# A segment-memory attention kernel: the memory update's products join the read-outs' transactions, the pair loop is written out, and Q and K are stored in runs of 8

## The chip, the core and the metric

The kernel runs on one core of a Trainium2 chip. Its engines are TensorE (PE, which multiplies and transposes), VectorE (DVE), ScalarE (ACT), GpSimd (POOL) and SyncE (SP, which issues DMAs). They run side by side and wait for each other through semaphores. The metric is the device time of one execution in microseconds, less is better.

## What is computed

A transformer block: attention with a memory carried over segments, then a coupled feed-forward net. The work around the change is the attention (input (8, 512, 256), 16 heads of 64, segments of 128 rows):

```python
def step(carry, seg):
    M, Z = carry
    scores = jnp.einsum('bhid,bhjd->bhij', q, k) * scale
    scores = jnp.where(mask, -jnp.inf, scores)
    att_dot = jnp.einsum('bhij,bhjv->bhiv', jax.nn.softmax(scores, axis=-1), v)
    sq = jax.nn.elu(q) + 1.0
    att_mem = sq @ M / (sq @ jnp.swapaxes(Z, -2, -1))
    sk = jax.nn.elu(k) + 1.0
    M_new = M + jnp.einsum('bhld,bhlv->bhdv', sk, v)
    Z_new = Z + sk.sum(axis=-2, keepdims=True)
    att = gate * att_mem + (1.0 - gate) * att_dot
    out = att.reshape(B, LSEG, H * DV) @ Wo
    return ((M_new, Z_new), out)
```

Before it stand a layer norm and the projections of x by Wq, Wk and Wv; behind it a layer norm and the residual sum. Then comes a feed-forward net over three cycles, again with norm and residual.

## The kernel before

The eight sequences are worked in four pairs, each over four segments: 16 steps (bp, s). One step handles 32 units (2 sequences x 16 heads) in 4 groups of 8. For pairs 0 to 2 each engine runs a loop (`Fori`) whose body holds the four steps of a pair; the last pair is written out behind it, without the parts that prepare further segments.

The order of the work is written by hand, as a function `step` for each engine, and each engine executes its own list in order. For each group g a step has `turn` (PE transposes the pairs of heads of Q and K), ACT's `take_q` and DVE's `take_q` (split into two f16 parts, and elu of Q), `scores` (PE, L1140 and L1145), `maxima` (DVE, L837), `probs` (ACT, eight exps, L576), `turn_probs` (PE, L1156), `take_p` (ACT, L582), two `read_out` halves (PE, L1169 for probabilities times V, L1174 for elu(Q) times memory), `divide` (DVE, L844 and L847) and `gated` (POOL, L420 to L424). Beside them the six projections of the next segment run (`project`, PE, L1111, 12 matmuls each). DVE turns each result in blocks from PSUM into Q, K or V (`take_x`, L816). The attention of the previous step is turned (`to_rows`, DVE, L913; `turn_att`, PE, L1201) and multiplied by Wo (`project_out`, PE, L1216, 32 matmuls); its norms are `y_norm` and `x2_norm` (DVE, L760), with POOL's `deviation` (L390, L392). N names the rows of a segment two steps ahead, F the rows that go to the feed-forward net.

The memory update is `exp_k` (ACT, L566, L569), `elu_k` (POOL, L404, L407) and `remember`: PE multiplies elu(K) by V (L1189) and DVE adds the product to M (L865). In segment 3 there is no update; DVE copies the start values into M (`reset`, L784).

PSUM has 8 banks. Two hold a projection's result (`x_bank`), two the scores and then the turned probabilities (`s_bank`), two the read-outs (`pm_bank`, 260 of 512 words each). The remaining two (`t_bank`) take turns for all other results, as jobs in the fixed order of `STEP_JOBS`: `turn` of Q and K, A0 to A3, Y, N, F, and the update's halves U0a to U3b. A job waits until DVE or ACT has freed its bank from the job before the last one (`t_free`). A read-out waits for pm_free, which `divide` raises.

Q and K lie in SBUF unit by unit, 64 words each (`p (u e)`), V in units of 68 words. `turn` takes two adjacent units, 128 words in a row. A unit pair holds heads 2j and 2j + 1.

At the start, SP issues eight DMAs of x, then Wq, Wk and Wv as one DMA each, and then the smaller inputs. ACT makes the weights' high f16 parts (`weights`, L517), DVE the low ones (`low_weights`, L792).

## Time and profile before

| | us |
|---|---|
| median of 3 runs | 1248.91 (1248.09 to 1250.15) |
| the profiled execution | 1248.27 |
| its span on the core, first to last instruction | 1246.5 |
| busy: PE, DVE, ACT, POOL | 1066.8, 823.6, 611.5, 586.0 |
| attention from the first to the last L1216 inside a step | 69.90 to 995.52 |
| last L1216, feed-forward net and outputs | 1049.62 to 1246.5 |

Times inside the profile are us from the start of the span. A busy share says how much an engine does, not whether the others wait for it. A timeline row stands for a group of instructions and names in brackets the idle time before it, with the engine and line that ended it. The ends of PE's matmuls are modelled, so neighbouring groups overlap by some 0.2 us; from start to start the lengths are exact. PEclk is the granted clock of PE as a share of full speed.

### The profile page before, as it was taken

To read this page: it belongs to the slowest core of one execution; us is meant where nothing else is said; L and a number is where in the kernel's file an instruction comes from. 1 tells how busy PE (TensorE), PEld (TensorE's weight loads), DVE (VectorE), ACT (ScalarE), POOL (GpSimd) and SP (SyncE) were. 2 spreads that over 40 slices of the span, in tenths; PEclk is the share of its full clock that TensorE was granted. 3 is DMA by queue.
4 is the path that set the end of the run, shared out by engine and by line. 5 is a ranking of instruction groups with operands and counts; after the bars stand their busy time and mean duration, and the time that the engine had idled before them with its cause. 6 is when DMAs were issued, how large, how long until landed. Compare 5 with 4: busy or idle time off the path is not lost.

```text
span 1246.5 us, 20616 instructions
## 1 busy us (share of the span) xinstructions
PE 1066.8 (86%) x7108; PEld 745.9 (60%) x7172; DVE 823.6 (66%) x1492; ACT 611.5 (49%) x1291; POOL 586.0 (47%) x715
## 2 busy tenths in 40 slices
PE   2898989887999898879999988898998879999972
PEld 1476767664767676647676766676767665433331
DVE  3868686865686868656867686768686652444375
ACT  3545454544454544544535445445454553566663
POOL 2145454554454545544545454545454551323266
PEclk9999999988999999989999999999999888999995
DMA  6100000000000000000000000000000010300014
GB/s 156 30 10 9 10 9 10 10 11 10 10 9 10 9 10 10 10 11 10 9 9 9 10 10 10 9 10 9 9 1 9 2 28 1 144 0 0 1 34 102
DMA packets 14954, 24.02 MB, mean 19 GB/s; under 512 B 5376, under 2 KB 7168, under 8 KB 14336
## 3 DMA queue, kind: packets, MB, share of 16 engines
q1 hardware_dynamic: 14848, 22.63, 6.3%
q8 instruction: 63, 1.03, 0.3%
q14 instruction: 43, 0.35, 0.1%
HBM read 13.97 MB, written 8.65 MB: 18 GB/s over the span
## 4 chain that ended last, share of the span: by engine, by line
PE 43%; DVE 31%; issue 11%; ACT 10%; POOL 2%; DMA 2%; DVEq 0%; SPq 0%; POOLq 0%; ACTq 0%
PE ps L1216 10%; DVE arena L816 9%; PE ps L1111 8%; PE ps L1329 6%; ACT arena L576 4%; PE ps L1169 4%; PE ps L1342 3%; PE ps L1156 3%; DVE arena L760 3%; DVE arena L847 2%; PE ps L1174 2%; DVE arena L865 2%; DVE arena L826 2%; DVE arena L830 2%; DVE arena L837 2%
## 5 line engine op out<-in xcount | busy, mean ns | idle before, releaser
L1111 PE MATMUL ps<-arena 128*128 128x512 f16 x1152 | 272.7, 388 | 8.2 <-DVE arena L792 5.4
L576 ACT ACTIVATE arena<-ps,arena 128x128 f32<-128x128 f32 x512 | 139.3, 383 | 226.6 <-DVE arena L837 226.3
L816 DVE STREAM_TRANSPOSE arena<-ps 128x1024 f32<-128x1024 f32 x96 | 190.3, 1985 | 42.1 <-PE ps L1111 42.1
L1111 PEld LDWEIGHTS ps<-arena 128*128 128x128 f16 x1152 | 113.3, 100 | 133.5 <-issue 19.1
L420 POOL TENSOR_TENSOR arena<-arena 128x256 f32<-128x256 f32 x128 | 93.1, 728 | 131.2 <-DVE arena L847 131.1
L1169 PEld LDWEIGHTS ps<-arena 128*128 128x128 f32 x1024 | 133.0, 198 | 29.1 <-issue 20.6
L1169 PE MATMUL ps<-arena 128*128 128x65 f32 x1024 | 136.6, 278 | 15.5 <-DVE arena L847 14.3
L404 POOL TENSOR_TENSOR arena<-arena 128x512 f32<-128x512 f32 x64 | 81.4, 1271 | 124.4 <-ACT arena L569 124.4
L1216 PE MATMUL ps<-arena 128*128 128x256 f32 x544 | 122.0, 382 | 0.3 <-ACT arena L588 0.3
L390 POOL TENSOR_TENSOR arena<-arena 128x2 f32<-128x2 f32 x50 | 9.8, 197 | 238.0 <-DVE arena L756 238.0
L1216 PEld LDWEIGHTS ps<-arena 128*128 128x128 f32 x544 | 102.0, 190 | 16.1 <-ACT arena L588 1.4
L752 DVE BATCH_NORM_STATS2 arena<-arena 128x6 f32<-128x256 f32 x100 | 36.7, 409 | 111.5 <-ACT arena L594 97.4
L1156 PE MATMUL ps<-arena 128*128 128x128 f32 x512 | 80.7, 294 | 32.1 <-ACT arena L576 31.8
L1189 PE MATMUL ps<-arena 128*128 128x130 f32 x384 | 66.0, 309 | 41.8 <-DVE arena L777 24.1
L424 POOL TENSOR_TENSOR arena<-arena 128x256 f32<-128x256 f32 x128 | 94.3, 737 | 10.0
L422 POOL TENSOR_TENSOR arena<-arena 128x256 f32<-128x256 f32 x128 | 93.2, 728 | 10.0
L847 DVE TENSOR_TENSOR arena<-ps,arena 128x512 f32<-128x512 f32 x128 | 88.5, 692 | 13.1 <-DVE arena L844 0.8
L582 ACT ACTIVATE arena<-ps 128x1024 f32<-128x1024 f32 x64 | 65.7, 1026 | 62.5 <-PE ps L1156 62.5
L760 DVE TENSOR_SCALAR arena<-arena 128x256 f32<-128x256 f32 x100 | 68.7, 728 | 37.1 <-POOL arena L392 37.1
L1156 PEld LDWEIGHTS ps<-arena 128*128 128x128 f32 x512 | 61.2, 150 | 49.5 <-ACT arena L576 48.5
L1174 PE MATMUL ps<-arena 128*128 128x130 f32 x512 | 90.3, 301 | 0.0
L837 DVE TENSOR_REDUCE arena<-ps 128x4 f32<-128x512 f32 x128 | 81.8, 679 | 12.8 <-PE ps L1145 12.4
(109 smaller groups left out, 1813.1 us busy)
## 6 DMA issues: line engine op xcount, KB each, us to landing
x_rows<-arena SPq DMA_DIRECT2D x17, 256.0 KB, 2.0
arena<-in_L_attn_x_dram SPq DMA_DIRECT2D x64, 64.0 KB
arena<-x_rows SPq DMA_DIRECT2D x4, 1024.0 KB, 8.1
out_dram<-arena SPq DMA_DIRECT2D x32, 128.0 KB, 2.8
arena<-in_L_attn_Wq_dram SPq DMA_DIRECT2D x1, 1024.0 KB, 13.8
arena<-in_L_attn_Wk_dram SPq DMA_DIRECT2D x1, 1024.0 KB, 18.9
arena<-in_L_attn_Wv_dram SPq DMA_DIRECT2D x1, 1024.0 KB, 22.5
arena<-in_L_attn_Wo_dram SPq DMA_DIRECT2D x8, 128.0 KB, 10.4
```

The lines of the kernel that those rows point to most:

```text
L422: pool.tensor_tensor(mem, mem, gt, ALU.mult).then_inc(mix, 1)
L424: pool.tensor_tensor(att.rearrange("p (e u) -> p u e", u=UNITS)[:, u:u + 4], mem, dot, ALU.add).then_inc(att_done, 1)
L576: last = act.activation(Pr[:, par, j, :], s_bank[:, par, j * P:(j + 1) * P], ACT.Exp, bias=negm[:, par, j:j + 1])
L760: last = dve.tensor_scalar(dst[:, w * D:(w + 1) * D], src[:, w * D:(w + 1) * D], mv[:, w, 0:1], rs[:, w:w + 1], ALU.subtract, ALU.mult)
L816: dve.transpose(dst[:, d0:d0 + 32, :], bank.rearrange("p w (d c) -> p d w c", c=C)).then_inc(x_free, 1)
L837: dve.tensor_reduce(negm[:, par, :], s_bank[:, par, :].rearrange("p (j i) -> p j i", j=GP), AX.X, ALU.max, negate=True).then_inc(m_done, 1)
L847: dve.tensor_tensor(AB[half], rd[:, :, :, 0:DK], rr.rearrange("p m (u a) -> p m u a", a=1).to_broadcast([P, 2, 4, DK]), ALU.mult).then_inc ...
L1111: last = pe.matmul(bank[:, w, :], xc[:, lx, k, w * P:(w + 1) * P], W16[lw][:, k, i, :], start=(n == 0), stop=(n == 5))
L1156: last = pe.transpose(s_bank[:, par, j * P:(j + 1) * P], Pr[:, par, j, :], identf)
L1169: pe.matmul(pm_bank[:, 0, u * DV1:(u + 1) * DV1], PT[:, par, j, :], v[:, GU * g + 2 * j + par, 0:DV1], start=True, stop=True)
L1174: last = pe.matmul(pm_bank[:, 1, a * 2 * DV1:(a + 1) * 2 * DV1], sqT[g % 2][:, j, :], M[:, GP * g + j, :, :], start=True, stop=True)
L1216: last = pe.matmul(t_bank[b][:, w * D:(w + 1) * D], attT[:, w, j, :], Wo_sb[:, j, :], start=(j == 0), stop=(j == 7))
```

## The change

- The jobs U0a to U3b, `remember` and `memory_stands` are gone. Each `read_out` half also multiplies its four units of elu(K) by V, into the unused words 260 to 519 of the two `pm_bank` banks, and raises pm_full once for all three. `divide` adds these products to M (or copies the start values in segment 3) before it raises pm_free. A read-out outside segment 3 waits for its group of elu(K).
- Read-out (3, 1) of a step stands behind the next step's `scores` 0, its `divide` behind the next `maxima` 0, and both `gated` of group 3 behind the next `elu_k` 0. Read-out (3, 0) stands ahead of `project` 5.
- DVE's and POOL's orders change; DVE's `take_k` is parted from `take_q`. ACT's and POOL's work on elu(K) falls away in segment 3.
- All 16 steps are written out on PE, DVE, ACT and POOL. SP keeps its loop.
- Q and K lie as `(v e h)`: four quarters (sequence, half of the heads), in each 64 rows of 8 heads. DVE's transposes write runs of 8 words. `turn`, `exp_k` and the first add of `elu_k` read words 8 apart; elu(K) itself is stored packed. A unit pair is now head h and head h + 8, in M, M0, V and the gate as well.
- At the start, ACT issues half of x's first tile and Wq and Wk, each in two halves, SP the rest and Wv in halves. ACT's `weights(0)` and DVE's `low_weights(0)` move ahead of the first rows' conversion. V's low parts are made by POOL.

The diff, cut to what the prediction speaks of:

```diff
-STEP_JOBS = ["Q1", "K1", "A0", "A1", "A2", "A3", "Y", "Q2", "K2", "N", "U0a", "U0b", "U1a", "U1b",
-             "Q3", "K3", "F", "U2a", "U2b", "Q0", "K0", "U3a", "U3b"]
...
+        def heads(a):
+            return a.rearrange("p (y z h) -> p y h z", y=2, h=HP)
+        def group(a, g):
+            return heads(a)[:, g // 2, GP * (g % 2):GP * (g % 2) + GP]
...
+        STEPS = [divmod(m, NSEG) for m in range(NT)]
+        def before(bp, s):
+            return STEPS[bp * NSEG + s - 1]
...
+                for dst, src in list(blocks(xrow[0], x_rows, 0, 0))[0:2]:
+                    sp.dma_start(dst, src).then_inc(x_in[0], 16)
+                for dst, src in blocks(xrow[1], x_rows, 0, 1):
+                    sp.dma_start(dst, src).then_inc(x_in[1], 16)
+                for k in range(KT):
+                    sp.dma_start(w_raw[2][:, k, :], Wv[k * P:(k + 1) * P, :]).then_inc(w_in[2][k], 16)
...
+                for dst, src in list(blocks(xrow[0], x_rows, 0, 0))[2:4]:
+                    act.dma_start(dst, src).then_inc(x_in[0], 16)
+                for i, w in enumerate((Wq, Wk)):
+                    for k in range(KT):
+                        act.dma_start(w_raw[i][:, k, :], w[k * P:(k + 1) * P, :]).then_inc(w_in[i][k], 16)
...
+                    if m > 0:
+                        gated(*before(bp, s), 3, 0)
+                        gated(*before(bp, s), 3, 1)
                     elu_k(bp, s, 1)
                     gated(bp, s, 0, 0)
                     gated(bp, s, 0, 1)
-                    if ahead:
-                        deviation(n_rs, n_mv, n_stat, n_rstd, bp * NSEG + (s + 3))
+                    if m < NT - 2:
+                        deviation(n_rs, n_mv, n_stat, n_rstd, m + 3)
                     y_dev(bp, s)
+                    gated(bp, s, 1, 0)
+                    residual(bp, s)
                     elu_k(bp, s, 2)
-                    residual(bp, s)
-                    gated(bp, s, 1, 0)
                     x2_dev(bp, s)
                     gated(bp, s, 1, 1)
                     elu_k(bp, s, 3)
                     gated(bp, s, 2, 0)
                     gated(bp, s, 2, 1)
-                    gated(bp, s, 3, 0)
-                    gated(bp, s, 3, 1)
...
+                    pool.tensor_tensor(pairs, pairs, group(k_pos[s % 2], g), ALU.add).then_inc(sk_part, 1)
...
+                    if s > 0:
+                        act.wait_ge(pm_full, bp * 32 + 8 * (s - 1) + 2 * g + 2)
+                    elif bp > 0:
+                        act.wait_ge(pm_full, (bp - 1) * 32 + 8 * (NSEG - 2) + 2 * g + 2)
+                    act.activation(part.rearrange("p (h z) -> p h z", h=GP), group(k_pos[s % 2], g), ACT.Relu,
+                                   scale=-1.0).then_inc(rk_done, 1)
...
+                    dst = (q_pos, k_pos, v_pos)[i // 2][par].rearrange(
+                        "p (u e) -> p e u" if i >= 4 else "p (v e h) -> p e v h", **(
+                            dict(u=UNITS) if i >= 4 else dict(v=UNITS // HP, h=HP)))
                     d0 = 32 * (i % 2)
...
-                    dve.tensor_tensor(AB[half], rd[:, :, :, 0:DK],
-                                      rr.rearrange("p m (u a) -> p m u a", a=1).to_broadcast([P, 2, 4, DK]),
-                                      ALU.mult).then_inc(pm_free, 1)
+                    last = dve.tensor_tensor(AB[half], rd[:, :, :, 0:DK],
+                                             rr.rearrange("p m (u a) -> p m u a", a=1).to_broadcast([P, 2, 4, DK]),
+                                             ALU.mult)
+                    j, j0 = GP * g + 2 * half, (GP * g + 2 * half) % (H // 2)
+                    T = pm_bank[:, :, 4 * DV1:6 * DV1].rearrange("p j (h e) -> p j h e", h=2)
+                    for par in range(2):
+                        p = slice(64 * par, 64 * par + 64)
+                        m = M[p, j:j + 2, par, :]
+                        if s < NSEG - 1:
                             last = dve.tensor_tensor(m, T[p, :, par, :], m, ALU.add)
-                        last.then_inc(t_free[b], 1)
+                        elif bp < PAIRS - 1:
+                            last = dve.tensor_copy(m, M0[p, j0:j0 + 2, :])
+                    last.then_inc(pm_free, 1)
...
                     maxima(bp, s, 0)
+                    if m > 0:
+                        divide(*before(bp, s), 3, 1)
                     if not last:
                         take_x(bp, s, 0)
                     to_rows(bp * 32 + 8 * s + 8)
                     take_q(bp, s, 1)
+                    take_k(bp, s, 1)
+                    divide(bp, s, 0, 0)
                     if not last:
                         take_x(bp, s, 1)
-                    divide(bp, s, 0, 0)
                     maxima(bp, s, 1)
                     divide(bp, s, 0, 1)
+                    if ahead:
+                        n_stats((s + 2) % 4, bp * 64 + 64 * (1 + (s + 2) // 4), m + 3)
                     if not last:
                         take_x(bp, s, 2)
                     if ahead:
-                        n_stats((s + 2) % 4, bp * 64 + 64 * (1 + (s + 2) // 4), bp * NSEG + (s + 3))
-                    if ahead:
-                        n_norm((s + 2) % 4, bp * NSEG + (s + 3))
+                        n_norm((s + 2) % 4, m + 3)
                     y_stats(bp, s)
                     take_q(bp, s, 2)
                     divide(bp, s, 1, 0)
+                    take_k(bp, s, 2)
                     y_norm(bp, s)
+                    maxima(bp, s, 2)
+                    if ahead:
+                        split(t_job(bp, s, "N"), s % 2, m + 3)
                     if not last:
                         take_x(bp, s, 3)
-                    if ahead:
-                        split(t_job(bp, s, "N"), s % 2, bp * NSEG + (s + 3))
-                    maxima(bp, s, 2)
-                    remember(bp, s, 0, last)
+                    x2_stats(bp, s)
                     divide(bp, s, 1, 1)
-                    remember(bp, s, 1, last)
-                    x2_stats(bp, s)
                     x2_norm(bp, s)
                     take_q(bp, s, 3)
+                    take_k(bp, s, 3)
+                    divide(bp, s, 2, 0)
+                    maxima(bp, s, 3)
+                    seq_sums(bp, s)
+                    divide(bp, s, 2, 1)
                     if not last:
                         take_x(bp, s, 4)
-                    divide(bp, s, 2, 0)
-                    seq_sums(bp, s)
-                    maxima(bp, s, 3)
-                    divide(bp, s, 2, 1)
-                    remember(bp, s, 2, last)
-                    if not last:
                         take_q(bp, s, 0)
+                        take_k(bp, s, 0)
                     divide(bp, s, 3, 0)
                     if not last:
                         take_x(bp, s, 5)
-                    divide(bp, s, 3, 1)
-                    remember(bp, s, 3, last)
...
-                            u = GU * g + 2 * j
                             last = pe.transpose(t_bank[b][:, j * P:(j + 1) * P],
-                                                src[par][:, u * DK:(u + 2) * DK], identf)
+                                                heads(src[par])[:, g // 2, GP * (g % 2) + j], identf)
                         last.then_inc(t_full[b], 1)
...
-                                  v[:, GU * g + 2 * j + par, 0:DV1], start=True, stop=True)
-                    memory_stands(pe, bp, s, g)
+                                  v[:, GP * (g % 2) + j, par, 0:DV1], start=True, stop=True)
+                    if bp == 0 and s == 0:
+                        pe.wait_ge(m_reset, 2 * (g + 1))
                     for a in range(2):
                         j = 2 * half + a
                         last = pe.matmul(pm_bank[:, 1, a * 2 * DV1:(a + 1) * 2 * DV1], sqT[g % 2][:, j, :],
                                          M[:, GP * g + j, :, :], start=True, stop=True)
+                    if s < NSEG - 1:
+                        pe.wait_ge(sk_done, sk_count(bp, s, g) + 2)
+                        for a in range(2):
+                            h = GP * (g % 2) + 2 * half + a
+                            last = pe.matmul(pm_bank[:, a, 4 * DV1:6 * DV1],
+                                             sk[:, 2 * DK * (GP * (g - g % 2) + h):
+                                                2 * DK * (GP * (g - g % 2) + h + 1)], v[:, h, :, 0:DV1],
+                                             start=True, stop=True)
                     last.then_inc(pm_full, 1)
-                def remember(bp, s, g):
...
                     scores(bp, s, 0)
+                    if m > 0:
+                        read_out(*before(bp, s), 3, 1)
                     if not last:
                         project(bp, s, 0)
                     turn_probs(bp, s, 0)
...
                     scores(bp, s, 2)
-                    remember(bp, s, 0)
                     read_out(bp, s, 1, 1)
-                    remember(bp, s, 1)
                     turn_probs(bp, s, 2)
                     turn(bp, s, 3)
                     if not last:
                         project(bp, s, 4)
                     read_out(bp, s, 2, 0)
-                    turn_rows(t_job(bp, s, "F"), row, x2n_done, bp * NSEG + (s + 1))
+                    turn_rows(t_job(bp, s, "F"), row, x2n_done, m + 1)
                     scores(bp, s, 3)
-                    remember(bp, s, 2)
                     read_out(bp, s, 2, 1)
                     turn_probs(bp, s, 3)
                     if not last:
                         turn(bp, s, 0)
+                    read_out(bp, s, 3, 0)
                     if not last:
                         project(bp, s, 5)
-                    read_out(bp, s, 3, 0)
-                    remember(bp, s, 3)
-                    read_out(bp, s, 3, 1)
```

## Rows read from the trace of the kernel before

**Rows 1.** The page's first part: busy us, share of the span, instructions.

```profile
PE 1066.8 (86%) x7108; PEld 745.9 (60%) x7172; DVE 823.6 (66%) x1492; ACT 611.5 (49%) x1291; POOL 586.0 (47%) x715
```

**Rows 2.** Windows between starts of L1216: bounds, length, busy per engine, PEclk, DMA.

```profile
254.40:322.02 67.62, 54.93 (x389) 39.89 (x394) 43.74 (x77) 29.94 (x67) 31.50 (x39) 0.87 0.03 10
...
504.69:571.39 66.70, 53.58 (x389) 39.03 (x394) 43.65 (x77) 29.94 (x67) 31.52 (x39) 0.90 0.03 10
...
632.60:693.63 61.03, 55.49 (x421) 42.45 (x426) 45.19 (x84) 29.83 (x67) 31.54 (x39) 0.97 0.03 10
...
754.44:814.79 60.35, 52.75 (x390) 39.33 (x394) 43.84 (x77) 29.82 (x67) 31.57 (x39) 0.94 0.03 10
814.79:876.26 61.47, 55.72 (x422) 42.45 (x426) 45.45 (x85) 29.83 (x67) 31.51 (x39) 0.97 0.03 9
...
937.77:995.52 57.75, 48.93 (x380) 39.37 (x384) 37.95 (x74) 29.05 (x67) 29.70 (x36) 0.94 0.02 6
```

**Rows 3.** The chain that ended last, 632.60 to 693.63: start, length, what.

```profile
632.60 7.05 PE ps L1216 x32
...
667.67 2.59 PE ps L1111 x12
670.26 0.84 PE ps L1169 x8
671.10 0.52 PE ps L1174 x4
...
692.75 0.87 PE ps L1156 x8
```

**Rows 4.** Timeline of PE, same window: start, length (end modelled), group, idle before.

```profile
644.93 0.38 PE L1140 MATMUL ps<-arena 128*128 128x512 bf16 x1
...
646.02 0.71 PE L1189 MATMUL ps<-arena 128*128 128x130 f32 x4
648.93 0.71 PE L1189 MATMUL ps<-arena 128*128 128x130 f32 x4 [2.20 <-DVE arena L777]
...
652.72 1.70 PE L1156 MATMUL ps<-arena 128*128 128x128 f32 x8
...
662.72 0.71 PE L1189 MATMUL ps<-arena 128*128 128x130 f32 x4 [1.21 <-DVE arena L895]
```

**Rows 5.** Timeline of DVE, same window.

```profile
643.75 0.20 DVE L844 RECIPROCAL arena<-ps 128x8 f32<-128x8 f32 x1
...
644.68 1.84 DVE L760 TENSOR_SCALAR arena<-arena 128x256 f32<-128x256 f32 x2
646.44 1.92 DVE L816 STREAM_TRANSPOSE arena<-ps 128x1024 f32<-128x1024 f32 x1
...
648.81 1.26 DVE L837 TENSOR_REDUCE arena<-ps 128x4 f32<-128x512 f32 x2
...
659.16 2.06 DVE L816 STREAM_TRANSPOSE arena<-ps 128x1024 f32<-128x1024 f32 x1
...
665.75 1.21 DVE L865 TENSOR_TENSOR arena<-ps,arena 64x130 f32<-64x130 f32 x4
```

**Rows 6.** Timeline of ACT, same window.

```profile
649.51 2.18 ACT L576 ACTIVATE arena<-ps,arena 128x128 f32<-128x128 f32 x8 [3.99 <-DVE arena L837]
```

**Rows 7.** Timeline of PE in the window from 754.44, which has no U jobs.

```profile
772.58 0.66 PE L1156 MATMUL ps<-arena 128*128 128x128 f32 x4 [3.10 <-ACT arena L576]
```

**Rows 8.** Groups by line and form: count, busy us, mean ns, idle before.

```profile
L816 DVE STREAM_TRANSPOSE arena<-ps 128x1024 f32<-128x1024 f32 x96 | 190.3, 1985 | 42.1 <-PE ps L1111 42.1
...
L913 DVE STREAM_TRANSPOSE arena<-arena 128x1024 f32<-128x1024 f32 x34 | 40.3, 1222 | 2.1 <-POOL arena L424 1.6
...
L792 DVE TENSOR_TENSOR arena<-arena 128x1024 f16<-128x1024 f32 x6 | 11.2, 1904 | 4.1 <-ACT arena L517 4.1
```

**Rows 9.** Timeline of PE where the pair loop jumps back the first time.

```profile
300.84 0.59 PE L1140 MATMUL ps<-arena 128*128 128x512 bf16 x1 [5.76 <-issue]
```

**Rows 10.** The chain that ended last, 0 to 70.

```profile
6.82 18.92 DMA arena<-in_L_attn_Wk_dram
```

178 lines of the change are left out of this document (73 added, 105 removed).

## The prediction

> **What bounds the kernel now.** I read the engines' totals first. PE is busy 1066.8 of 1246.5 us, DVE 823.6, ACT and POOL half of the span [rows 1]. These are shares of a whole, so I cut the attention phase at the starts of L1216 (the output projection), once per step [rows 2]. A normal window between two such starts takes 60.8 to 61.5 us; there are eleven, of which [rows 2] shows two, and their mean is 61.2. The three windows that start in segment 3 take 67.62, 66.70 and 60.35, and the window from 937.77, which has no rows to prepare ahead, 57.75. FFN and tail, after 1049.62, run through code that the change leaves alone.
>
> Then the work of PE in a window, by the true lengths that the chain gives to PE when it leads [rows 3]: 6 projections of 12 matmuls at 2.59, one output projection 7.05, 8 read-outs at 0.84 + 0.52, 11 groups of eight transposes (4 of probabilities, 4 of Q and K, 2 of att, the rows of N and F together one) at 0.87, 4 score groups at 1.09 (start of L1140 at 644.93 to the next start at 646.02 [rows 4]). The products of the memory update are 4-matmul groups of the shape of L1174, 0.52 each, 8 in a window. Sum: 15.5 + 7.05 + 10.9 + 9.6 + 4.4 + 4.2 = 51.6 us. So 61.2 holds 9.6 us in which PE has nothing to do. PE is not the bound; it is the engine whose holes are worth filling.
>
> PE's timeline shows the holes [rows 4]. Before 648.93 it waits 2.20 us for DVE's L777: U0b needs the transposition bank that job N holds until `split`. Before 662.72 it waits 1.21 for L895 in the same way: U2b needs F's bank. The modelled ends of matmuls hide about 0.2 more in each. The shared banks are thus 3.8 of the 9.6, and U1b ahead of the transposes at 652.72 waits for the adds of U0b besides. DVE's order is behind the first: after the scores of group 2 end at 646.8, DVE goes through `y_norm` (1.84), `take_x` 3 (1.92) and `split`, and only at 648.81 comes to `maxima` [rows 5], from which ACT's exps (2.18 for a group of eight [rows 6]) and the transposes follow.
>
> **A window without U jobs shows that freeing the banks alone gives nearly nothing.** From 754.44 no U job runs. PE has 4.2 us less to do and no bank to wait for, yet the window takes 60.35. Its hole is a new one: 3.10 us ahead of the transposes at 772.58, for ACT's exps [rows 7], since `maxima` still stood behind `take_x` and `split`. Part of the rest is a clock that fell after that hole: granted 0.94 over the window instead of 0.97 to 1.00 [rows 2]. So what the change gives depends on its new DVE order more than on the banks.
>
> **The change part by part.**
>
> *U jobs into the read-outs' banks, new order.* Nothing is removed from PE, 51.6 stays. DVE's four adds per group (1.21 for four, 0.30 each [rows 5]) now stand inside `divide`, ahead of pm_free, so a read-out's bank comes free 0.6 later: `divide` is 0.93 (start 643.75 to 644.68) + 0.6 = 1.55 instead of 0.93. I laid the new order out over the same lengths, from the end of L1216 (t = 0). Q2's turn, read-out (1,0), K2's turn, project 3 and N's rows end at 6.6. DVE frees K2 at 5.9, so the scores run to 7.7. `maxima` stands now ahead of `split` and `take_x`, ends at 9.1 after `y_norm`, and the transposes of group 2 begin at 9.6 and end at 11.2; before, they began only 13.1 after the end of L1216 (652.72 less 632.60 + 7.05). Those of group 3 end at 22.4, of the next step's group 0 at 35.0, of group 1 at 49.4, and there the next L1216 starts, 56.5 from start to start. That is 51.6 of work, 3.5 for the strided transposes (below) and 1.4 of holes that remain. What comes late next is DVE's queue: `take_k` 2, `divide` (2,0) with its adds ahead of read-out (2,1), and `to_rows`, which must wait for POOL's `gated` (3,1), now begun only after the next step's first scores; behind `to_rows` on DVE stand `take_q` 1, `take_k` 1 and scores 1. I add 1.0 for semaphore and contention delays that such a layout leaves out. Window: 57.5.
>
> *Q and K in runs of 8.* DVE's four Q/K transposes each window write single words a column of heads apart (L816, 1985 ns). L913 moves as many words and writes runs of 16 at 1222 ns [rows 8]. Runs of 8 lie nearer to L913: 0.76 x 4 = 3.1 us less on DVE, bounds 0 and 3.1. DVE isn't the bound over the window, so this is in the layout and not added to it; without it the layout ends some 0.5 to 1 later. The price is on the readers: PE's transposes, ACT's Relu of K and POOL's first add now read words 32 bytes apart. No PE instruction of the trace reads so. The nearest row is DVE's L792, 1904 ns for 1024 words read far apart, against 1222 packed [rows 8], or about 1.7 ns a word instead of 1.0. If PE needs 1.7 ns a word as well, 128 words take 0.22 us and not the 0.109 (0.87 / 8) of now: 32 transposes x 0.11 = 3.5 us more a window. The other bound is 0. I take the price, because L816 is as slow for V (2.06 us at 659.16, words 272 bytes apart) as for K (1.92 at 646.44, 256 apart) [rows 5], so it is a matter of packed or not, not of one step size. Most of it falls into holes in which PE would wait for DVE or ACT: my layout gives 55.1 + 1.0 without the price and 56.5 + 1.0 with it, so 1.4.
> The Trainium skill (SBUF — State Buffer, "Door 1: The DMA port swizzle") speaks against the change here: SBUF is read in lines of 16 bytes, and accesses that each meet a new line pay. By that rule PE pays the price, and the window is the 57.5 of my forecast; without it 56.1. For DVE the trace agrees (1904 against 1222), for PE no row shows it.
>
> *Pair loop written out.* PE sat 5.76 us before L1140 at 300.84 with nothing awaited but "issue" [rows 9]; that is the jump back, and the window from 504.69 holds it a second time. The exit to the straight last pair has no such hole, and a straight window (814.79, 61.47) is no faster than looped ones (61.03). So the gain is the two jumps, 5.8 each, and nothing elsewhere. Bounds: 11.6 less, and 5 less if the straight windows' 0.44 more (61.47 against 61.03) is a price of straight code that fifteen windows then pay; I take 11.6, since looped windows reach 61.5 as well.
>
> *Segment-3 windows.* They have no U products (47.4 us of work), but DVE copies the start values in the adds' place, so DVE's path is the same. I take 54.5, three below a normal one: less than 4.2, since in the window of rows 7 only part of the missing work became time.
>
> *Last read-out behind the next scores.* It fills PE while DVE and ACT do `maxima` and the exps; this is inside the layout. At the very end one read-out and one `divide` come after the step as before: 0.
>
> *Start.* The transfer of Wk is the longest piece of the whole chain, 6.82 to 25.74 [rows 10]. Its issue moves from behind eight x issues on SP to ACT's queue behind two, in halves, and Wq is converted before the first rows. V's low parts go from DVE to POOL, idle there: two pieces of 1.9 (L792) leave DVE's path, but POOL may need longer, and project 4 then waits for POOL. All bytes share the same engines. Bounds 0 and 10; I take 6, some 4 for the earlier issue and 2 for DVE.
>
> **Sum.** 11 x (61.2 - 57.5) = 40.7; 67.62 + 66.70 + 60.35 - 3 x 54.5 = 31.2 (11.6 of it the jumps); 57.75 - 54.0 = 3.7; start 6. Together 81.6. The profiled execution took 1248.27 with a span of 1246.5, so 1166.7 for such an execution; the median of the runs is 0.6 above it: 1167 us.
>
> **Rivals.**
> *No price on PE* (0.22): 1.4 less in eleven windows and about 1.2 in four: 20 us, 1147. For it: PE is another reader than DVE, and no row shows it paying.
> *New waits take the banks' place* (0.25): the layout is too kind. POOL's `elu_k` reads K strided and stands ahead of `gated` (3,*), `to_rows` waits for that, and every DVE instruction behind it with it; and each bank release carries 0.6 more of adds. For it speaks the window of rows 7, where a freed wait came back at once. A delay of 2.2 in each of 15 windows is 33 us: 1200.
> *Slower* (0.03): PE's strided transposes. The forecast has room for 82 us, that is 5.4 in each of 15 windows, or 0.17 us for each of the 32 transposes beyond 0.22, if nothing more is hidden. From 0.39 us a transpose, three and a half times now's, the kernel is slower; at 0.42 it would be 1262. Against it: even DVE's far words cost 1.7 times packed ones, not 3.5.
> *It does little* (0.03): DVE's order loses what PE's gains, only jumps and start remain: 1248.9 - 11.6 - 6 = 1231.
> The forecast itself, 1155 to 1185, has 0.47.
>
> **Range.** Down to 1138 for no price and a full start gain (1147 less 4, and some 5 for fewer delays than 1.0 a window), up to 1204 for the new waits with a little more. Faster by over 0.2%, 0.95; within 0.2% (2.5 us, about what a measurement of this kernel can tell from no change) 0.02; slower 0.03.
>
> **What would show it.** In the profile after: no PE wait for L777 or L895's successors; no 5.8 us "issue" hole at 300 and 550; windows between output projections near 57.5, with no segment-3 window above them; the Q/K transposes on DVE near 1.2 us with V's still near 2.0; PE's loads and transposes of Q and K at 0.22 each if the price is real, 0.11 if not; L1216's first start some 6 us earlier. The forecast is wrong upward if `to_rows` or pm_free appear as waits of over 2 us a window, and downward if PE's turns are unchanged.

## The result and the profile after

The changed kernel takes 1136.7 us (median of 4 runs, 1134.37 to 1141.15), the kernel before 1248.6 beside it on the same chip: a ratio of 0.910 (95% interval 0.907 to 0.913). Forecast were 1167 with a range of 1138 to 1204. The sign and most of the mechanism held; the gain was 112 us where 82 were forecast, and it fell just out of the low end.

First part of the page of after, and the shares of the chain that ended last:

```profile
PE 1024.0 (90%) x7108; PEld 724.1 (64%) x7172; DVE 778.0 (69%) x1514; ACT 617.8 (55%) x1259; POOL 561.6 (50%) x685
...
PE 76%; ACT 9%; DVE 8%; issue 2%; DMA 2%; POOL 2%; SPq 0%; POOLq 0%; ACTq 0%; DVEq 0%
```

PE has the same 7108 instructions as in [rows 1], and 90% of the span instead of 86%. The chain tells it better: PE is now three quarters of it. The output projection is L1230 in after. The stretches between its starts, as windows (bounds, length, busy per engine, PEclk, DMA), beside [rows 2]:

```profile
0.00:68.78 68.78, 38.77 (x247) 23.37 (x250) 38.01 (x57) 32.80 (x51) 24.08 (x36) 1.00 0.31 85
...
231.29:287.90 56.61, 52.04 (x397) 38.48 (x402) 43.26 (x84) 28.55 (x63) 26.77 (x36) 0.97 0.03 11
450.38:506.68 56.30, 52.13 (x398) 38.83 (x402) 43.27 (x84) 28.54 (x63) 26.76 (x36) 0.97 0.03 10
561.08:615.50 54.42, 53.01 (x422) 40.82 (x426) 42.02 (x83) 31.87 (x67) 32.43 (x40) 1.00 0.03 11
615.50:669.18 53.68, 52.10 (x413) 39.94 (x418) 42.11 (x84) 28.57 (x63) 27.08 (x36) 1.00 0.03 11
669.18:724.56 55.38, 50.61 (x398) 38.16 (x402) 43.26 (x84) 28.54 (x63) 26.80 (x36) 1.00 0.03 10
833.37:886.54 53.17, 46.30 (x374) 37.24 (x377) 35.44 (x69) 27.91 (x63) 24.84 (x32) 0.97 0.02 6
886.54:934.97 48.43, 40.75 (x243) 30.50 (x245) 19.98 (x47) 21.34 (x45) 17.39 (x25) 0.93 0.08 19
```

The eleven normal windows have a mean of 54.2. The three that start in segment 3 are the longest (56.61, 56.30, 55.38), 1 to 2 us over a normal one of 54.4. Before, two of them were the longest by some six microseconds (67.62, 66.70), and the third was shorter than a normal one (60.35). The account of the 114.3 us between the two profiled spans (1246.5 and 1132.2), against the sum of the prediction:

| piece | forecast | measured |
|---|---|---|
| 11 normal windows | 40.7 | 76.9 |
| 3 segment-3 windows | 31.2 | 26.4 |
| the window with no rows to prepare | 3.7 | 4.6 |
| start, to the first output projection | 6 | 1.1 |
| last window of the attention | 0 | 5.7 |
| feed-forward net and outputs | 0 | -0.4 |

So the question is one of the normal windows. PE's timeline inside one of them, as [rows 4] (start, length with modelled end, group, idle before):

```profile
576.13 0.66 PE L1196 MATMUL ps<-arena 128*128 128x130 f32 x4
576.63 0.61 PE L1202 MATMUL ps<-arena 128*128 128x130 f32 x4
577.22 0.66 PE L1177 MATMUL ps<-arena 128*128 128x128 f32 x4
578.25 0.66 PE L1177 MATMUL ps<-arena 128*128 128x128 f32 x4 [0.37 <-ACT arena L607]
578.74 1.05 PE L1149 MATMUL ps<-arena 128*128 128x128 f32 x8
579.63 2.75 PE L1133 MATMUL ps<-arena 128*128 128x512 f16 x12
...
588.81 0.66 PE L1177 MATMUL ps<-arena 128*128 128x128 f32 x4 [0.38 <-ACT arena L607]
...
590.58 1.11 PE L1190 MATMUL ps<-arena 128*128 128x65 f32 x8 [0.23 <-ACT arena L613]
```

These and one of 0.28 ahead of the scores at 574.10 are all the idle gaps that the timeline names in the window, 1.3 us together; before, a single one had 2.20. The three shown are waits for the second half of the exps (L607) or for the copy of the turned probabilities (L613); for the one of 0.28 the view names only "issue". None is a wait for a bank. L1202, the memory update's product, stands right behind L1196 and needs no bank of its own. The chain gives the true lengths, as in [rows 3]:

```profile
569.41 0.50 PE ps L1196 x4
569.91 0.45 PE ps L1202 x4
...
578.91 0.88 PE ps L1149 x8
...
582.38 0.84 PE ps L1190 x8
...
596.43 1.04 PE ps L1190 x8
```

The turn of eight pairs (L1149), which reads words 32 bytes apart, takes 0.88, where the layout of before took 0.87. The read-out L1190 takes 0.84 behind a projection, but 1.04 behind the scores: pieces of 0.2 like this one, and the modelled ends around each wait, are presumably the rest of the 3.2 us of idling that the count of PE's work leaves over (54.2 less 51.0; they were not added up one by one). And the groups by line and form (count, busy us, mean ns, idle before):

```profile
L839 DVE STREAM_TRANSPOSE arena<-ps 128x1024 f32<-128x1024 f32 x96 | 146.2, 1523 | 27.7 <-PE ps L1133 25.4
...
L423 POOL TENSOR_TENSOR arena<-arena 128x512 f32<-128x512 f32 x48 | 73.1, 1522 | 107.7 <-ACT arena L600 107.7
L1149 PEld LDWEIGHTS ps<-arena 128*128 128x128 f32 x512 | 65.1, 191 | 2.2 <-issue 1.2
L596 ACT ACTIVATE arena<-arena 128x512 f32<-128x512 f32 x48 | 54.5, 1135 | 0.0
```

The 1523 of L839 is a mean of two kinds, which DVE's timeline of the same window parts: a Q/K tile, then a V tile.

```profile
577.10 1.24 DVE L839 STREAM_TRANSPOSE arena<-ps 128x1024 f32<-128x1024 f32 x1
...
589.32 2.12 DVE L839 STREAM_TRANSPOSE arena<-ps 128x1024 f32<-128x1024 f32 x1
```

### The profile page after: what moved, and what is told of

Read it like the earlier page. It is cut to its first block, busy times and chain, and to the rows that moved or that the text cites. A ratio compares the mean times of both kernels' runs of the same rounds, so it can differ in the third digit from the quotient of the medians.

```text
span 1132.2 us, 18929 instructions
## 1 busy us (share of the span) xinstructions
PE 1024.0 (90%) x7108; PEld 724.1 (64%) x7172; DVE 778.0 (69%) x1514; ACT 617.8 (55%) x1259; POOL 561.6 (50%) x685
## 4 chain that ended last, share of the span: by engine, by line
PE 76%; ACT 9%; DVE 8%; issue 2%; DMA 2%; POOL 2%; SPq 0%; POOLq 0%; ACTq 0%; DVEq 0%
PE ps L1133 21%; PE ps L1230 11%; PE ps L1190 7%; PE ps L1340 7%; ACT arena L607 6%; PE ps L1177 4%; PE ps L1166 4%; PE ps L1196 4%; PE ps L1149 4%; PE ps L1353 3%; PE ps L1215 3%; PE ps L1202 3%; DVE arena L864 2%; PE ps L1161 2%; DMA arena<-in_L_attn_x_dram 2%
## 5 line engine op out<-in xcount | busy, mean ns | idle before, releaser
L1133 PE MATMUL ps<-arena 128*128 128x512 f16 x1152 | 267.8, 383 | 1.7 <-DVE arena L839 1.7
L607 ACT ACTIVATE arena<-ps,arena 128x128 f32<-128x128 f32 x512 | 138.9, 382 | 130.8 <-DVE arena L864 130.5
L839 DVE STREAM_TRANSPOSE arena<-ps 128x1024 f32<-128x1024 f32 x96 | 146.2, 1523 | 27.7 <-PE ps L1133 25.4
L1190 PE MATMUL ps<-arena 128*128 128x65 f32 x1024 | 136.1, 276 | 10.4 <-ACT arena L613 4.7
L1190 PEld LDWEIGHTS ps<-arena 128*128 128x128 f32 x1024 | 128.2, 193 | 23.4 <-ACT arena L613 8.0
L423 POOL TENSOR_TENSOR arena<-arena 128x512 f32<-128x512 f32 x48 | 73.1, 1522 | 107.7 <-ACT arena L600 107.7
L1230 PE MATMUL ps<-arena 128*128 128x256 f32 x544 | 122.0, 382 | 0.3 <-ACT arena L619 0.3
L1230 PEld LDWEIGHTS ps<-arena 128*128 128x128 f32 x544 | 102.0, 190 | 16.1 <-ACT arena L619 1.4
L613 ACT ACTIVATE arena<-ps 128x1024 f32<-128x1024 f32 x64 | 65.6, 1025 | 54.7 <-PE ps L1177 54.7
L1177 PE MATMUL ps<-arena 128*128 128x128 f32 x512 | 76.2, 282 | 15.8 <-ACT arena L607 15.8
L1340 PE MATMUL ps<-arena 128*128 128x512 f32 (+1 forms) x192 | 87.5, 599 | 0.8 <-ACT arena L718 0.8
L1196 PE MATMUL ps<-arena 128*128 128x130 f32 x512 | 86.2, 291 | 0.0
L493 POOL TENSOR_TENSOR arena<-arena 128x512 f32<-128x512 f32 (+1 forms) x22 | 37.6, 1708 | 96.8 <-DVE arena L1028 96.8
L1027 DVE TENSOR_TENSOR arena<-arena 128x512 f32<-128x512 f32 x24 | 29.4, 1225 | 77.7 <-ACT arena L709 77.7
```

The costliest lines, as they stand in the source:

```text
L607: last = act.activation(Pr[:, par, j, :], s_bank[:, par, j * P:(j + 1) * P], ACT.Exp, bias=negm[:, par, j:j + 1])
L839: dve.transpose(dst[:, d0:d0 + 32], bank.rearrange("p w (d c) -> p d w c", c=C)).then_inc(x_free, 1)
L1133: last = pe.matmul(bank[:, w, :], xc[:, lx, k, w * P:(w + 1) * P], W16[lw][:, k, i, :], start=(n == 0), stop=(n == 5))
L1177: last = pe.transpose(s_bank[:, par, j * P:(j + 1) * P], Pr[:, par, j, :], identf)
L1190: pe.matmul(pm_bank[:, 0, u * DV1:(u + 1) * DV1], PT[:, par, j, :], v[:, GP * (g % 2) + j, par, 0:DV1], start=True, stop=True)
L1196: last = pe.matmul(pm_bank[:, 1, a * 2 * DV1:(a + 1) * 2 * DV1], sqT[g % 2][:, j, :], M[:, GP * g + j, :, :], start=True, stop=True)
```

## The experiments

Each run is compared with the kernel before on its own chip; the changed kernel stands at 0.910 (0.907 to 0.913) by the same measure. A difference of two ratios of 0.01 is 12.5 us, and each ratio has an interval of 2 to 5 us to either side, so differences of some 5 us rest on the windows and not on the ratios. Windows are taken between the starts of the output projection.

**e1: PE's turns read packed words.** Does PE pay for the strided read?

```diff
-heads(src[par])[:, g // 2, GP * (g % 2) + j], identf)
+src[par][:, (GU * g + 2 * j) * DK:(GU * g + 2 * j + 2) * DK], identf)
```

> The changed kernel, but PE's transposes of Q and K read 128 words in a row instead of words 8 apart (so they transpose other words, and the output is not the reference's); all else writes and reads as in the changed kernel. Prediction on record: the strided read costs 0.11 us a transpose, some 1.4 to 3.5 us a window; packed again the kernel would be 20 to 50 us faster than the changed one (1136.7), 1087 to 1117. Rival, from the trace after: the loads are longer (191 against 148 ns) but lie under the matmul before them, groups of eight still take 0.88, so nothing changes: 1136.7 within 2, with loads of L1149 back at 148 ns.

0.9097 (0.9061 to 0.9134): no difference from the changed kernel. Normal windows 54.39 and 53.60, against 54.41 and 53.69. The one row that moved is the loads', by groups:

```profile
L1149 PEld LDWEIGHTS ps<-arena 128*128 128x128 f32 x512 | 59.6, 142 | 3.0 <-issue 1.2
```

A load of strided words takes 191 ns and one of packed words 142, but loads run beside matmuls, and the group of eight starts and ends at the same distances. The price is not hidden in holes; it does not reach the matmuls at all (e11 below shows that time added to PE's turns would be seen). The forecast's reason for 57.5 falls.

**e2: Q and K back in the old layout.** The pairing of heads goes back with it, all else is as changed: what are the runs of 8 worth?

```diff
-"p (u e) -> p e u" if i >= 4 else "p (v e h) -> p e v h", **(
-    dict(u=UNITS) if i >= 4 else dict(v=UNITS // HP, h=HP)))
+"p (u e) -> p e u", u=UNITS)
...
-a.rearrange("p (y z h) -> p y h z", y=2, h=HP)
+a.rearrange("p (y h z) -> p y h z", y=2, h=HP)
```

> The changed kernel with Q and K stored unit by unit and adjacent heads paired, as before the change; everything else stays. DVE's Q/K transposes go from 1.26 back to 1.98 us (2.9 more a window), ACT's Relu from 1.13 to 0.62, POOL's first add from 1.52 to 1.27. If the runs of 8 carry part of the gain, the windows grow from 54.4 by 1 to 3 us and the kernel by 15 to 45, 1152 to 1182. Rival: DVE has slack and PE leads the chain, so at most 0.3 a window: 1134 to 1142.

0.9202 (0.9176 to 0.9228), so the layout is worth about 13 us. Groups, and PE's timeline with a wait that the changed kernel lacks:

```profile
L838 DVE STREAM_TRANSPOSE arena<-ps 128x1024 f32<-128x1024 f32 x96 | 193.4, 2015 | 22.0 <-PE ps L1132 20.3
...
L596 ACT ACTIVATE arena<-arena 128x512 f32<-128x512 f32 x48 | 29.8, 620 | 0.0
```

```profile
555.06 2.76 PE L1132 MATMUL ps<-arena 128*128 128x512 f16 x12 [0.38 <-DVE arena L838]
```

Windows are 55.50 and 54.88 where they were 54.41 and 53.69, 1.1 more. The segment-3 windows are 55.5, no longer than the normal ones. DVE's share of the chain rises from 8% to 20%. ACT and POOL pay for the runs of 8 (620 to 1135 ns, 1273 to 1522 ns), and neither is on the chain with it.

**e3: maxima 2 back behind `split` and `take_x` 3.** The banks stay freed.

```diff
-maxima(bp, s, 2)
+if not last:
+    take_x(bp, s, 3)
 if ahead:
     split(t_job(bp, s, "N"), s % 2, m + 3)
-if not last:
-    take_x(bp, s, 3)
+maxima(bp, s, 2)
```

> The changed kernel, but DVE does take_x 3 and split ahead of maxima 2, in the order of before. If the new order is what makes the freed banks worth anything, PE waits some 2 to 3 us for ACT's exps in each of 16 windows, and the kernel takes 1165 to 1180. If the banks alone carry the gain: within 5 of 1136.7.

0.924 (0.9208 to 0.9272), 17.6 us over the changed kernel. Only this one move of DVE's new order is taken back. The hole comes back at its place, in PE's timeline:

```profile
533.75 0.66 PE L1177 MATMUL ps<-arena 128*128 128x128 f32 x4 [1.16 <-ACT arena L607]
```

Normal windows are 55.58 and 54.83 where they were 54.41 and 53.69, the segment-3 ones 57.95, 56.46 and 58.10.

**e4: the update's products back in the two shared banks.** The new order and all else stay.

```diff
-STEP_JOBS = ["Q1", "K1", "A0", "A1", "A2", "A3", "Y", "Q2", "K2", "N", "Q3", "K3", "F", "Q0", "K0"]
+STEP_JOBS = ["Q1", "K1", "A0", "A1", "A2", "A3", "Y", "Q2", "K2", "N", "U0a", "U0b", "U1a", "U1b",
+             "Q3", "K3", "F", "U2a", "U2b", "Q0", "K0", "U3a", "U3b"]
...
 scores(bp, s, 2)
+remember(bp, s, 0)
 read_out(bp, s, 1, 1)
+remember(bp, s, 1)
```

> The changed kernel, but the products of the memory update are jobs U0a to U3b of the two transposition banks again, with DVE's adds behind the matching divide and the last pair's behind the next step's first divide; loops, layout and all other orders stay as changed. If the banks carry most of the gain of 7 us a window, 15 windows less three of segment 3 give back 4 to 6 each: 1185 to 1210. If the order carries it, at most 1.5 each: 1137 to 1155.

0.9486 (0.9459 to 0.9513): 48 us more, the largest single part. PE's timeline in one window:

```profile
545.95 0.71 PE L1230 MATMUL ps<-arena 128*128 128x130 f32 x4 [1.34 <-DVE arena L807]
...
551.02 1.34 PE L1164 MATMUL ps<-arena 128*128 128x128 f32 x8 [1.25 <-DVE arena L896]
...
559.91 0.71 PE L1230 MATMUL ps<-arena 128*128 128x130 f32 x4 [1.34 <-DVE arena L926]
...
563.50 1.34 PE L1164 MATMUL ps<-arena 128*128 128x128 f32 x8 [0.66 <-DVE arena L896]
```

Here L1230 is the update's product, L1164 the turn of Q and K, and the four waits are for banks: 4.6 us, and 4.1 is what the window of 58.48 has over 54.41. So the waits for the banks become time nearly one for one once DVE's order lets PE run.

**e5: the kernel before with its pair loop written out, and nothing else.**

```diff
-with pe.Fori(0, PAIRS - 1) as bp:
+for bp in range(PAIRS - 1):
```

> The kernel before with the pair loop written out on PE, DVE, ACT and POOL, nothing else. Prediction on record: two jumps of 5.8 us go, nothing elsewhere: 1237. Rivals: straight code costs 0.4 a window: 1243; or the jumps hid other work that is then late: 1245 or more.

0.9836 (0.9804 to 0.9868), 20.5 us less. The segment-3 window, to be laid beside the 67.62 of [rows 2]:

```profile
253.66:312.19 58.53, 51.58 (x389) 38.45 (x394) 43.85 (x77) 29.83 (x67) 31.56 (x39) 0.97 0.03 10
```

Its PEclk is 0.97 where the looped window had 0.87, and PE's busy time 51.58 instead of 54.93. The two windows with a jump lost 9.1 (67.62 to 58.53) and 7.7 us (66.70 to 59.01): the 5.8 of the jump itself, and another 3.3 and 1.9. In the first these 3.3 are what PE's busy time lost with the same 389 matmuls, so they are matmuls that ran longer at the fallen clock; in the second that explains 1.1 of the 1.9 (53.58 to 52.51 busy). The third, which had no jump, went from 60.35 to 59.20. Behind the jump at 300.84 the windows view of the kernel before reads

```profile
300.80:312.00 11.20, 10.84 (x69) 6.07 (x68) 6.17 (x7) 6.15 (x15) 0.31 (x1) 0.77 0.01 1
```

and is back at 1.00 in the ten us after. The normal windows of e5 stay at 60.3 to 62.1, so straight code has no price.

**e6: the kernel before with maxima 2 moved ahead, and nothing else.**

```diff
 y_norm(bp, s)
-if not last:
-    take_x(bp, s, 3)
+maxima(bp, s, 2)
 if ahead:
     split(t_job(bp, s, "N"), s % 2, bp * NSEG + (s + 3))
-maxima(bp, s, 2)
+if not last:
+    take_x(bp, s, 3)
```

> The kernel before with one move on DVE: maxima 2 ahead of split and take_x 3. The order alone: PE's 2.2 us wait for split in front of U0b stays or grows by the 1.2 of maxima, the exps come 2.5 earlier. If order alone pays: 2 us in each of 16 windows, 1215. If the banks hold PE back first: within 8 of 1248.6, either way.

0.9968 (0.9941 to 0.9995, 10 runs): some 4 us. The normal windows go from 61.2 to 60.9 in the mean. In PE's timeline of the window from 569.5 the waits for the banks of U0b and U2b are still there (1.63 for L777 and 1.33 for L895, where [rows 4] has 2.20 and 1.21):

```profile
585.40 0.71 PE L1189 MATMUL ps<-arena 128*128 128x130 f32 x4 [1.63 <-DVE arena L777]
```

The transposes of group 2 begin at 589.65, which is 13.1 us after the end of L1216, as before. The exps came 2.2 us sooner in their window, but PE was held by the banks. The same move is worth 17.6 us in e3 and 4 here.

**e7: the last read-out back at the end of its step.**

```diff
 if not last:
     project(bp, s, 5)
+read_out(bp, s, 3, 1)
...
 scores(bp, s, 0)
-if m > 0:
-    read_out(*before(bp, s), 3, 1)
```

> The changed kernel with read-out (3, 1), its divide and both gated of group 3 back at the end of their own step. If the move fills PE while the maxima and exps of the next step run, its loss costs 1 to 2 us a window: 1150 to 1170. Rival: to_rows starts earlier, since gated is done earlier, and that pays for it: 1133 to 1142.

0.9138 (0.911 to 0.9167), about 5 us more; the two intervals overlap a little, and the windows show what changed. It is two effects of opposite sign. Normal windows grow by 0.8 (55.24 and 54.41), which is 9 us in eleven. The segment-3 windows shrink to 54.17, 54.15, 54.17. DVE's timeline there:

```profile
267.11 0.45 DVE L882 COPY arena<-arena 64x130 f32<-64x130 f32 x2
```

In the changed kernel one pair of these copies takes 2.52, with POOL's and PE's rows around it:

```profile
264.14 1.52 POOL L423 TENSOR_TENSOR arena<-arena 128x512 f32<-128x512 f32 x1 [2.79 <-ACT arena L600]
...
265.74 1.26 POOL L425 TENSOR_TENSOR arena<-arena 128x512 f32<-128x512 f32 x1
```

```profile
264.56 2.52 DVE L885 COPY arena<-arena 64x130 f32<-64x130 f32 x2
...
270.98 0.45 DVE L885 COPY arena<-arena 64x130 f32<-64x130 f32 x2
```

```profile
267.23 1.08 PE L1190 MATMUL ps<-arena 128*128 128x65 f32 x8 [1.52 <-DVE arena L885]
...
269.21 4.21 PE L1133 MATMUL ps<-arena 128*128 128x512 f16 x12 [0.40 <-DVE arena L839]
```

The copies end as POOL's two adds of `elu_k` end, at 267.0, and the bank is released behind them. PE waits 1.52, and the projection that follows takes 4.21 instead of 2.75. The windows view gives the granted clock of that stretch:

```profile
267.20:273.20 6.00, 5.57 (x24) 3.00 (x25) 4.18 (x7) 2.17 (x8) 3.70 (x6) 0.72 0.00 0
```

In the third segment-3 window the clock did not fall (1.00), and it is 55.38 and not 56.3 to 56.6: the clash alone costs some 2 us there, against the 53.4 of e9 below, and the clock another 1.

**e8: x ahead of the weights.** ACT's queue takes half of x's second tile.

```diff
-for dst, src in blocks(xrow[1], x_rows, 0, 1):
+for dst, src in list(blocks(xrow[1], x_rows, 0, 1))[0:2]:
     sp.dma_start(dst, src).then_inc(x_in[1], 16)
...
+for dst, src in list(blocks(xrow[1], x_rows, 0, 1))[2:4]:
+    act.dma_start(dst, src).then_inc(x_in[1], 16)
```

> The changed kernel with the second tile of x issued in halves on SP's and ACT's queues, ahead of all weights. In the trace after, that tile landed at 26.2 us (before: 16.5), and everything up to 30 us waited for it. If this ate the start's gain, the tile lands by 16, the first L1230 starts 4 to 7 us earlier, and the kernel takes 1130 to 1133. Rival: the weights are later by as much: 1136.7 within 1.

0.9148 (0.9114 to 0.9183), some 6 us slower, against what I expected. x's second tile lands at 22.0 instead of 26.2, but Wq at 27.5 instead of 15.2. The first output projection starts at 74.1, and the chain of the start has another head:

```profile
4.81 22.72 DMA arena<-in_L_attn_Wq_dram
```

**e9: the start values copied by ACT.** DVE's copies go, ACT makes them from the same source, ahead of its Relu of K; PE's read-outs of segment 0 wait for them.

```diff
-elif bp < PAIRS - 1:
-    last = dve.tensor_copy(m, M0[p, j0:j0 + 2, :])
...
 elif bp > 0:
-    act.wait_ge(pm_full, (bp - 1) * 32 + 8 * (NSEG - 2) + 2 * g + 2)
+    act.wait_ge(pm_full, (bp - 1) * 32 + 8 * (NSEG - 1) + 2 * g + 2)
+    for par in range(2):
+        p = slice(64 * par, 64 * par + 64)
+        act.activation(M[p, GP * g:GP * g + GP, par, :],
+                       M0[p, GP * g % (H // 2):GP * g % (H // 2) + GP, :],
+                       ACT.Copy).then_inc(m_reset, 1)
```

> The changed kernel, but after segment 3 the start values are copied into M by ACT, group by group ahead of its Relu of the next step, and not by DVE inside divide. In the trace after, the copies (L885) of one divide took 2.5 us while POOL was in gated, PE waited 1.5 for them and its clock then fell, so that segment-3 windows (56.6, 56.3, 55.4) are longer than those with more work (54.4). If that is it: these three windows fall to 53 to 54 and the kernel by 7 to 9: 1128 to 1130. Rival: the holes of segment 3 come from elsewhere, or ACT is late in the next step: 1135 to 1139.

0.9023 (0.8992 to 0.9053), some 9.5 us less. The segment-3 windows, with PEclk back at 1.00:

```profile
232.63:286.05 53.42, 50.77 (x401) 38.17 (x402) 38.72 (x72) 30.21 (x67) 26.31 (x35) 1.00 0.03 11
```

The other two are 53.41 and 53.42, so the three windows give 56.61 + 56.30 + 55.38 less 160.25, that is 8.0 us. With e7, whose pairs of copies take 0.45 each and whose segment-3 windows are the short ones, the clash is shown from two sides.

**e10: Wv behind Wq.**

```diff
+sp.wait_ge(w_in[0][KT - 1], 16)
 for k in range(KT):
     sp.dma_start(w_raw[2][:, k, :], Wv[k * P:(k + 1) * P, :]).then_inc(w_in[2][k], 16)
```

> The changed kernel, but SP waits until Wq has landed before it issues Wv and all that follows it. Issuing x first made the start longer by 5.5 us, since Wq then landed at 27.5. If the start is bound by bytes that are asked for too early, the second tile of x and Wq land by 15 to 18 here, and the first L1230 starts 5 to 8 earlier than at 68.8: 1129 to 1132. Rival: Wv or Wo is then late and takes it back: 1135 to 1140.

0.9074 (0.9037 to 0.9112), whose interval takes in the changed kernel's ratio, so no gain is shown for the whole kernel. The start does get shorter: the first output projection starts at 65.4 instead of 68.7, and x's second tile lands at 22.5 where it landed at 26.2. The profiled span is longer all the same (1134.9 against 1132.2), most of it by the last window (53.4 against 48.4, see below). The chain of the start of after, then of e10:

```profile
4.34 21.84 DMA arena<-in_L_attn_x_dram
26.20 0.75 DVE arena L781 x2
...
30.23 11.93 PE ps L1133 x48
```

```profile
4.32 18.19 DMA arena<-in_L_attn_x_dram
```

**e11: each turn of Q and K made twice.** PE gets 3.5 us more to do per window and nobody else any.

```diff
-for j in range(GP):
+for j in [*range(GP), *range(GP)]:
```

> The changed kernel with each of PE's transposes of Q and K done twice (same result): 32 more a window at 0.11 us, 3.5 us of PE work. My layout had most of such an addition fall into holes (1.4 of 3.5). If so: 15 to 25 us in all, 1152 to 1162. If PE has become the bound, nearly all of it shows: 3.2 to 3.5 in each of 16 windows, 1185 to 1193.

0.9411 (0.938 to 0.9442), 39 us slower. Windows are 57.29 and 56.38 where they were 54.41 and 53.69: of the added 3.5 (four groups at 0.88) 2.9 became time in the first kind and 2.7 in the second, between the two cases that I had expected. PE is the bound now, all but for some 0.6 to 0.8.

**e12: e9 and e10 together.** Their two diffs, nothing more.

> The edits of e9 (reset on ACT) and e10 (Wv asked for after Wq has landed) together. e9 took the three segment-3 windows to 53.4 and the kernel to 0.9023 of before; e10 moved the first L1230 from 68.8 to 65.5, while its median did not show it. If both hold and the rest stays: first L1230 near 65.5 and 0.900 of before, 1125 to 1128. Rival: what e10 gains at the start is given back at the end, where PE's clock varies from run to run: 0.902 to 0.904, 1128 to 1131.

1126.4 us (median of 5 runs, 1123.69 to 1128.39), 0.8987 (0.8969 to 0.9006): faster than both kernels. It is 14 us below the changed one by the ratios, 10 by the two medians, beside which the kernel before took 1248.6 and 1253.1. The segment-3 windows are 53.4 again; the first output projection starts at 67.0 and not near the 65.5 that I expected. First part of its page:

```profile
PE 1024.8 (91%) x7108; PEld 725.8 (64%) x7172; DVE 762.0 (68%) x1466; ACT 627.5 (56%) x1283; POOL 561.1 (50%) x685
```

## Why the prediction was right and wrong, step by step

**The parts, taken back one by one.** Banks 48 (e4), order of `maxima` 17.6 (e3), layout 13 (e2), last read-out 5 (e7), the loop 20 (e5, seen from the kernel before), start about 1: 105 of the 112 us. That they nearly add up is not more than a hint that no large part was missed, since e3 and e6 show that one part can depend on another. The order in this sum is one move of `maxima`; the rest of DVE's and POOL's new orders was not taken back.

**Step that failed first: the price of the strided turns.** I took 0.22 us for each of PE's 32 transposes from DVE's L792 and wrote that most of it falls into holes and 1.4 remain. It is 0.11 as before (L1149 x8 in 0.88), and e1 gives the same time with packed reads. The row I leaned on was of another engine and of another kind: in DVE's instruction the reading is the work, in PE's turn it is a load beside other matmuls. Even for DVE it was no clean price of the stride, since L792 subtracts two inputs from SBUF and L913 turns one. My second assumption, that most of such a price falls into holes (1.4 of 3.5 remain), fails as well: of the 3.5 that e11 adds at the same places 2.9 remain. I had named the case without a price as a rival with 0.22 and 1147; by its mechanism it was the true one, and the time came out 10 below even that.
Here the rule of the Trainium skill (SBUF — State Buffer, "Door 1: The DMA port swizzle") that separate 16-byte lines cost is borne out where the reading is the instruction: ACT 620 to 1135 ns, POOL 1273 to 1522, PE's load 142 to 191. The rule says nothing of whether the reading is on the path, and that of PE's loads isn't.

**The layout was right in mechanism and a size off.** Without the price my layout gave 55.1 + 1.0. The windows have 54.2. Two terms were too large. The products of the update are 0.45 a group (L1202) and not the 0.52 of L1174, 8 a window, so 0.6 less of work: 51.0. The other 3.2 are holes, where the layout had 3.5 and then 1.0 added for delays that it had left out, 1.3 too much. With the 1.4 of the price that makes 3.3 a window, and in eleven windows the 36 us that I was short.

**"Freeing the banks alone gives nearly nothing", and "it depends on its new DVE order more than on the banks": refuted, as far as was run.** Taking back the move of `maxima` costs 17.6 us (e3), taking back the banks 48 (e4). The window of [rows 7] did show that a wait for the exps appears when the banks are free, 3.10 there, and e3 reproduces it, but as 1.16. What I missed is what a freed bank is worth once the order is right: four waits, 4.6 us, in e4's window. It is the order alone that gives next to nothing, 4 us (e6), the reverse of what I wrote. A version of before with the banks alone was not run; e3 comes nearest, and it has the other parts of the change too.
A detail of my reading of the old window was off as well: the scores of group 2 end at 646.1 (L1145, 645.25 + 0.84), not at 646.8, and `y_norm` had begun at 644.68, so what stood between them and `maxima` was the end of `y_norm`, `take_x` 3 and `split`.

**The new waits (1200, 0.25): did not come.** No wait of PE's in a normal window reaches 0.5 us. `to_rows` (L933 in after) waits for POOL's `gated` five times in the whole span, 5.1 us together and 2.5 at most, and PE isn't behind it. The one place where the added work inside `divide` did hold a bank was segment 3, and there through a partner that I hadn't named.

**Segment-3 windows: the direction right, the reason incomplete.** Forecast 54.5 each, measured 56.61, 56.30, 55.38. I wrote that DVE copies the start values in the adds' place, so that its path is the same. It is not. The adds read PSUM and SBUF (0.58 for two, in every step); the copies read SBUF alone and stood still for as long as POOL's adds ran (2.52 for two instead of 0.45). e9 gives 53.42 when ACT copies. For this clash the trace agrees with the Trainium skill (SBUF — State Buffer, "Who interferes with whom"): a copy on VectorE in its two-port mode and a GpSimd instruction exclude each other, and whoever comes first holds the ports to its end. Here the first copy ends 0.08 after POOL's first add, the second 0.08 after its second. For one POOL instruction the trace doesn't bear this rule out: beside L403 (two words a partition, 0.70, at 249.68) a pair of copies takes its 0.45, as far as POOL's times can be trusted. I had read that page of the Trainium skill only for the strided read.

**The loop: right in place, too small.** I priced the two jumps at 5.8 each by [rows 9] and gained 11.6 from them. e5 gives 20.5. The surplus of 8.9 is PE's clock to about one half (3.3 and 1.1 in the two windows); for the rest (0.8 in the second window, 1.2 in the third segment-3 window, 2.0 in the eleven normal ones together, and what the runs differ by) no cause is shown. In [rows 2] the granted clock of those windows stood at 0.87 and 0.90, and I used that row only for the length. In the forecast it didn't cost me anything, since I set all three windows to 54.5 whatever was in them. The Trainium skill (Runtime: NRT & Kernel Launch, "Instruction fetch mechanics") says that a taken branch out of the prefetched pages forces a fetch before the engine goes on; the hole of 5.76 with "issue" as its reason agrees, and its disappearance in e5 too. That page of the Trainium skill gives no time for it.

**Start: 6 forecast, 1.1 measured.** I took the chain's head, Wk until 25.74 [rows 10], as what an earlier issue shortens. It was shortened, and x became the late one: in after x lands at 26.2. The first transfers compete, and the time at which each is asked for does not settle the order: x's second tile was asked for at 2.3 to 4.3 on SP's queue and landed at 26.2, Wk at 3.9 and 4.5 on ACT's queue and landed at 23.0. e10 shows the competition by sending Wv later (x's tile 3.7 sooner), and e8 from the other side: x sooner made Wq later (27.5), and the first output projection 5.4 later. How the two queues are served no run shows.
The 1.1 itself is hardly more than noise: over the profiles of the changed kernel, e1 to e4, e7 and e9, none of which edits the order of the first transfers, the first output projection starts at 68.0 to 70.0, and in those of before, e5 and e6 at 69.8 to 71.3. The 65.4 of e10, the 67.0 of e12 and the 74.1 of e8 lie outside.

**The last window: 0 forecast, 5.7 in this profile.** Its length varies by execution: 48.4 in this one of the changed kernel, 53.4 in e1's, e9's and e10's, none of which has an edit there but for the words that e1's turns read. Over all profiles it goes with the granted clock of the window: 48.4 at 0.93, 50.1 at 0.90 (e8), 52.2 at 0.87 (e12), 53.0 to 54.1 at 0.81 to 0.84 (the others, the kernel before among them). Timeline of PE and windows view, after first, then e1:

```profile
920.10 3.68 PE L1340 MATMUL ps<-arena 128*128 128x512 f32 x8
...
918.00:924.00 6.00, 5.68 (x27) 3.50 (x27) 2.45 (x9) 1.13 (x3) 4.38 (x6) 1.00 0.00 0
```

```profile
923.65 5.17 PE L1340 MATMUL ps<-arena 128*128 128x512 f32 x8
...
916.20:928.70 12.50, 11.30 (x36) 8.04 (x36) 4.64 (x11) 2.84 (x6) 5.07 (x7) 0.59 0.00 0
```

In e1 the groups are longer by the clock, granted 0.59 against 1.00, in both behind waits of 1.11 and 1.12 us. So some 5 of the 114 us between the two profiles are that one execution's. How many of the runs behind the median had them stays open. The mean clocks of the four runs on record (0.976 and 0.977 for the two shorter ones, 0.972 and 0.971 for the two longer) only hint at two. It also sets what a run can settle: the runs of the changed kernel spread over 6.8 us.

**What was right.** PE's instructions stayed the same and its holes were filled. No hole at a jump is left. The Q/K transposes take 1.24 with V's at 2.12, forecast 1.2 and 2.0. The remaining holes are those that the layout placed, behind the exps of groups 2 and 3. That the layout of Q and K had an indirect worth of "0.5 to 1" a window is 1.1 in e2.

**The range.** The low end took the missing price, a full start gain and some 5 us for smaller delays. The layout's own allowances were too large by more than that (1.3 for holes and delays, 0.6 of work, 21 us in eleven windows). They outweigh the 5 us each that the start and the segment-3 windows fell short, and put 1136.7 below 1138. That it came out on this side of 1138 is in part chance: 1.3 us is less than the last window varies by. The 3.3 us a window are not chance.

## What to carry to other kernels

A price for an access pattern counts only where that instruction is on the path: ask first what runs beside it. When holes of the leading engine are to be filled, take each known wait back by itself in a layout (bank, order, layout of data): here one move in DVE's order was worth 4 us in the kernel before and 18 in the new one, beside 48 for the banks and 13 for the layout. And a hole costs more than its length where PE's granted clock falls behind it, so read the clock of the window as part of the price.
